# Maxima transposed in 64x64 tiles, self placement in two halves, cross scores in three units, on one Trainium2 core

## The chip, the cores and the metric

The kernel runs on one core of a Trainium2 chip. The metric is the device time of one execution, in microseconds. Three runs of the kernel before gave 484.20, 483.22 and 483.26 us, with a median of 483.26. In the profile, PE is TensorE (PEld its weight loads), DVE is VectorE, ACT is ScalarE, POOL is GpSimd and SP is SyncE; a q behind a name is that engine's sequencer, which also issues DMAs.

## What is computed

The reference is two transformer layers over x, of shape 4x512x128. Layer 0 is causal self attention with normalised q and k, cross attention to a context of 154 rows (16 heads of 8 features each), and a gated mixture of 8 experts. Layer 1 is causal linear attention, a second cross attention with 8 heads of 128 features, and a feed-forward block of 384 hidden features.

```python
def _L0_attn_ref(x, W_qkv, q_scale, k_scale, W_out):
    qkv = jnp.einsum('bsd,de->bse', x, W_qkv)
    q, k, v = jnp.split(qkv, 3, axis=-1)
    q = _layernorm(q, q_scale)
    k = _layernorm(k, k_scale)
    ...
    scores = jnp.einsum('bshd,bthd->bhst', q / jnp.sqrt(Hd).astype(q.dtype), k)
    scores = jnp.where(future[None, None, :, :], jnp.finfo(scores.dtype).min, scores)
    attn = jax.nn.softmax(scores, axis=-1)
...
x = _layernorm(x + _L0_attn_ref(...), axis=-1)
x = _layernorm(x + _L0_xattn_ref(x, ctx_1024, ctx_1024, ...), axis=-1)
x = _layernorm(x + _L0_ffn_ref(...), axis=-1)
x = _layernorm(x + _L1_attn_ref(...), axis=-1)
x = _layernorm(x + _L1_xattn_ref(x, ctx_1024, ...), axis=-1)
x = _layernorm(x + _L1_ffn_ref(...), axis=-1)
```

## The kernel before

Work is cut into steps such as (b, "S", a, g, u): batch b, self (a = 0) or cross (a = 1) attention, group g of four heads, unit u. One program-wide list of steps is written out by hand: `MERGE` is a string of letters, each of which takes the next step of one stream (s scores, t transposed scores, p products, r preparation of a batch, l placement, u setup, and so on), and `BANK_OF` gives each step its PSUM bank or its pair of banks. Every engine walks this list and does its own part of each step, in that order. Semaphores count how often a bank was filled and drained. So a table decides what each engine has queued behind what.

Attention of layer 0 runs in turns, one for each (b, a, g), in the order `TURNS`. In a turn TensorE makes the scores S in units, and VectorE reduces each unit to its negated row maxima. The maxima are cut into three bf16 parts in `mparts`; the step mT transposes these on TensorE, ScalarE copies the result to `mrows`, and SyncE places it by one DMA into the rows `MAX_ROWS` of Q6. Then TensorE makes the transposed scores ST, from which the placed rows have already taken the maxima, ScalarE takes exponentials into EX, PV multiplies them with the values, and cT transposes the products back for the division. Cross scores of a turn are eight pieces of 128 query rows by 154 context rows, two pieces to a unit, so four units; self scores are five units. Both use TensorE in tiles of 64x64.

Q and k enter as bf16 triples (a value, its rest and the rest of that) so that bf16 products are exact enough. After the step qkT, ScalarE and VectorE make the three parts of 128x512. A placing step then copies parts by DMA into every eighth partition of the operands Q6 and K6: twelve DMAs of 128 KB to a batch, six for q and six for k (`shares`, `placement`, `place_self`). At batch 0 SyncE issues six and ScalarE the other six (`place_first`), and the first scores wait for all twelve.

The head of the program loads x, the weights and the context (SyncE's list `early`, 15 loads, then the expert biases), computes qkv of batch 0, and makes setup transposes (wT) and products (wM) of weights. The first of these, wT 0 to 3, transpose the context of a batch. `keep_busy` puts a few products without use in front of the first x0T and the first qkv.

## Time and profile before

| | before |
|---|---|
| median of three runs | 483.26 us |
| the profiled execution's own time | 484.66 us |
| its span, first to last instruction | 482.9 us |
| granted TensorE clock, mean over the span | 0.975 |
| TensorE busy | 449.9 us (93%) |
| VectorE busy | 381.7 us (79%) |
| ScalarE busy | 346.9 us (72%) |
| GpSimd busy | 187.2 us (39%) |
| instructions | 14117 |

The profile is of one execution. A busy time is the sum over an engine's instructions; on TensorE these overlap and their ends are modelled, so a full TensorE isn't one at its peak. A stretch table gives each engine's busy time and number of instructions in a window, with the granted clock as a share of full speed, the share of time that the DMA engines are busy, and GB/s. In a timeline a row is start, duration, engine, line, operation, output and input, count, and in brackets the idle time before it with what ended it. A row of several instructions lasts from the first start to the last end.

### The profile page before, as it was taken

The page shows a single profiled execution, that of the slowest core. Times are in us where ns is not written, and L with a number is a line of the kernel's source. Part 1 is how long each engine was busy: PE and PEld are TensorE (multiplying, and loading weights), DVE is VectorE, ACT ScalarE, POOL GpSimd, SP SyncE. Part 2 cuts the span into 40 slices and gives each one's busy share as a digit, 9 for nine tenths or more (in the row PEclk, how much of TensorE's full clock was granted, in tenths as well). Part 3 has the DMA queues.
Part 4 walks back from the last instruction along what each step waited for, and adds up shares of the span by engine and source line. Part 5 has one row for each costly group of instructions (what it writes and reads, how often), then busy time and mean ns, then how long its engine had stood idle before and what let it go on. Part 6 is the DMA issues. An engine that isn't in the chain of part 4 may idle for free.

```text
span 482.9 us, 14117 instructions
## 1 busy us (share of the span) xinstructions
PE 449.9 (93%) x5296; PEld 303.5 (63%) x5296; DVE 381.7 (79%) x1083; ACT 346.9 (72%) x879; POOL 187.2 (39%) x356
## 2 busy tenths in 40 slices
PE   5767889998999999999999999999999999999995
PEld 4534446654555546656778555668774765896984
DVE  2469897898899999898698988867879687764566
ACT  1635676976868878888667788996867878869642
POOL 7284000680202364434142252335334538644532
PEclk8677999999999999999999999999999999999999
DMA  7481210034200201131100000030000000000001
GB/s 230 99 209 32 76 46 5 24 89 105 60 13 14 68 2 39 39 92 34 37 4 13 13 3 4 3 76 19 3 13 14 1 1 2 1 1 1 2 12 33
DMA packets 27191, 18.50 MB, mean 38 GB/s; under 512 B 8217, under 2 KB 26773, under 8 KB 26997
## 3 DMA queue, kind: packets, MB, share of 16 engines
q1 hardware_dynamic: 23413, 15.44, 12.1%
q10 hardware_dynamic: 3712, 2.17, 1.9%
q8 instruction: 43, 0.70, 0.6%
q14 instruction: 23, 0.19, 0.1%
HBM read 5.58 MB, written 1.05 MB: 14 GB/s over the span
## 4 chain that ended last, share of the span: by engine, by line
PE 46%; DVE 4%; ACT 2%; POOL 1%; issue 1%; POOLq 0%; DVEq 0%; ACTq 0%
PE psum L1070 6%; PE psum L1452 6%; PE psum L1429 5%; PE psum L1463 3%; PE psum L1365 3%; PE psum L1149 2%; PE psum L1474 2%; PE psum L1176 2%; PE psum L1219 2%; PE psum L1203 2%; PE psum L1454 1%; PE psum L1321 1%; PE psum L1326 1%; PE psum L1373 1%; PE psum L1207 1%
## 5 line engine op out<-in xcount | busy, mean ns | idle before, releaser
L1600 ACT ACTIVATE EX<-psum 128x1024 f32<-128x1024 f32 (+1 forms) x128 | 119.3, 975 | 7.2 <-PE psum L1131 4.2
L1873 DVE TENSOR_REDUCE mparts<-psum 128x2 f32<-128x768 f32 (+1 forms) x96 | 77.5, 862 | 3.4 <-PE psum L1131 3.0
L1868 DVE TENSOR_REDUCE mparts<-psum 128x4 f32<-128x616 f32 (+1 forms) x80 | 68.0, 877 | 4.8 <-PE psum L1149 3.6
L1028 POOL TENSOR_TENSOR GP<-REST,xrs 128x512 f32<-128x512 f32 (+1 forms) x48 | 34.6, 743 | 48.8 <-DVE xrs L2100 24.8
L1149 PE MATMUL psum<-K,Q 64*64 64x154 bf16 (+8 forms) x1024 | 48.1, 266 | 4.9 <-DVE mparts L1873 2.2
L1176 PE MATMUL psum<-Q,K 64*64 64x512 bf16 (+7 forms) x640 | 42.9, 313 | 3.4 <-DVE mparts L1873 1.5
L1689 ACT ACTIVATE REST<-psum,nxmax 128x154 f32<-128x154 f32 x96 | 36.2, 393 | 9.2 <-DVE nxmax L2090 8.2
L1149 PEld LDWEIGHTS psum<-K,Q 64*64 64x64 bf16 x1024 | 22.3, 106 | 28.0 <-issue 14.4
L1219 PE MATMUL psum<-EX,V 128*32 128x256 f32 (+3 forms) x512 | 37.8, 435 | 1.2 <-ACT EX L1600 1.2
L954 POOL TENSOR_SCALAR rstd_rest<-moments_rest 128x2 f32<-128x2 f32 x32 | 7.3, 228 | 73.2 <-DVE moments_rest L1908 72.8
L954 POOL TENSOR_SCALAR rstd_attn<-moments_attn 128x4 f32<-128x4 f32 x8 | 1.9, 238 | 82.1 <-DVE moments_attn L1908 82.1
L2090 DVE TENSOR_REDUCE nxmax<-psum 128x2 f32<-128x308 f32 x64 | 28.9, 470 | 4.6 <-PE psum L1429 4.1
L1429 PE MATMUL psum<-GP,xT 128*128 128x308 f32 x96 | 30.3, 431 | 0.1
L1176 PEld LDWEIGHTS psum<-Q,K 64*64 64x64 bf16 x640 | 15.4, 105 | 19.1 <-issue 5.6
L1219 PEld LDWEIGHTS psum<-EX,V 128*32 128x32 f32 x512 | 15.1, 109 | 18.8 <-issue 15.8
L1615 ACT COPY pvraw<-psum 128x512 f32<-128x512 f32 x16 | 9.4, 587 | 21.1 <-PE psum L1219 20.9
L1452 PE MATMUL psum<-VM,REST 128*128 128x128 f32 x192 | 23.8, 277 | 0.3 <-ACT EX L1600 0.2
L957 POOL TENSOR_TENSOR rstd_rest<-rstd_rest,power 128x2 f32<-128x2 f32 x32 | 22.9, 715 | 2.7
L1452 PEld LDWEIGHTS psum<-VM,REST 128*128 128x128 f32 x192 | 22.5, 192 | 1.1 <-issue 0.6
L1365 PE MATMUL psum<-ew,xT 128*128 128x512 f32 x48 | 22.7, 607 | 0.0
L1070 PE MATMUL psum<-ident,X 128*128 128x128 f32 x90 | 17.6, 294 | 5.1 <-DMA Y_rest<-in_ctx 3.7
L1070 PE MATMUL psum<-ident,pvraw 128*128 128x128 f32 x128 | 20.0, 279 | 1.4 <-ACT EX L1600 1.1
(344 smaller groups left out, 1151.3 us busy)
## 6 DMA issues: line engine op xcount, KB each, us to landing
Q<-xparts SPq DMA_DIRECT2D x24, 128.0 KB
Q<-parts SPq DMA_DIRECT2D x21, 128.0 KB
K<-parts SPq DMA_DIRECT2D x21, 128.0 KB
X<-in_x SPq DMA_DIRECT2D x4, 256.0 KB, 3.1
Q<-in_L_xattn_Wkv SPq DMA_DIRECT2D x1, 1024.0 KB, 7.2
K<-xkparts SPq DMA_DIRECT2D x24, 38.5 KB
out<-XB_rest SPq DMA_DIRECT2D x6, 128.0 KB, 1.8
Q<-in_L_xattn_Wq SPq DMA_DIRECT2D x1, 512.0 KB, 4.3
```

What stands on the lines that cost most here:

```text
L1028: last = nc.gpsimd.tensor_tensor(of.XP[:, at:at + 4 * n].rearrange("p (h c) -> p h c", h=4)[:, :, 0:c1 - c0], of.XE[:, :, c0:c1], of.xrs.r ...
L1070: last = nc.tensor.transpose(to[0:n, at:at + m], src, ident[0:m, 0:m])
L1149: last = mm(to[half, r, at:at + n], Q6[a][p, b % 2, 2 * g + jj, P * q + TILE * e:P * q + TILE * e + TILE], K6[a][p, b % 2, 2 * g + jj, 0:n ...
L1176: last = mm(to[half, r, at + q - P * k:at + S - P * k], K6[a][p, b % 2, 2 * g + jj, P * k + TILE * e:P * k + TILE * e + TILE], Q6[a][p, b ...
L1219: last = mm(to[32 * h:32 * h + 32, P * k:S], V[:, k, 4 * g + h, :], EX[:, ex_slot(b, a, g, u) + h % 2, at:at + n], start=k == PV_ORDER[0], ...
L1365: fills_(mm(fill(key), half_of(b, h).xT[2][:, P * i:P * i + P], ew[:, 4 * side:4 * side + 4, :].rearrange("p e d -> p (e d)")), key)
L1429: fills_(mm(fill(key)[:, 0:2 * C], half_of(b, h).xT[4][:, P * q:P * q + P], G[:, head:head + 2, :].rearrange("p h c -> p (h c)")), key)
L1452: mm(to, of.XPT[:, head, :], VM[:, head, :], start=head == 0, stop=False)
L1600: drains(nc.scalar.activation(dst, src, ACT.Exp), key)
L1689: last = nc.scalar.activation(of.XE[:, i, :], src[:, C * j:C * j + C], ACT.Exp, bias=of.nxmax[:, i:i + 1], accum_out=of.xsum[:, i:i + 1])
L1868: last = vec.tensor_reduce(nmax[:, :, :, q], src[:, :, 0:2 * n].rearrange("p r (j k) -> p r j k", j=2), AX.X, ALU.max, negate=True)
L1873: last = vec.tensor_reduce(nmax[:, :, jj, q], src[:, :, at:at + P * (q + 1)], AX.X, ALU.max, negate=True)
```

## The change

- The maxima of a turn are transposed by two 64x64 products with `ident2` (one for each half of the partitions), not by one transpose against a bf16 identity. `mrows` holds the two results at partitions 0 to 47 and 64 to 111, and two DMAs place them. The counts of `max_placed` double.
- Cross scores are cut into units of three, three and two pieces of 154 columns, and VectorE reduces a unit of cross scores by one instruction.
- The features of q and k are put in the order half, parity, feature, head, so that each half of the partitions holds the heads of two groups. A placement of a part becomes two DMAs of 64 partitions. At batch 0 the first halves go first (`first_placed`, six by SyncE and six by ScalarE), and the scores of groups 0 and 1 wait for these alone; SyncE issues the twelve second halves in the last placing step, and group 2 waits for them.
- Five of the 15 early loads and the two loads of the expert biases are issued in that last placing step, ahead of its second halves. The late loads of ScalarE are issued at batch 1's step qkT of q, not at its last qkv.
- The transposed gates `gT` and the biases `eb` have all 128 rows, with zeros below row 16, so the product of the gate biases runs over 128 rows.
- `cT` is cleared only in its last 32 columns, the bf16 identity goes, and one memset of `mparts` goes.
- `MERGE` and `BANK_OF` are new. The new order begins x0T, qkv 0 to 3, qkT 0 and 1 of batch 0, then wT 0; before, wT 0 stood ahead of qkv 0 and wT 1 to 5 ahead of qkT. Its moments of batch 1 stand behind the five units of the first scores; before, ahead of them.

```diff
-X_PIECES = [[(0, 0, q), (C, 1, q)] for q in range(NB)]
+X_COUNT = P * NB // C
+X_PIECES = [[(C * (i - first), i // NB, i % NB) for i in range(first, min(first + X_COUNT, 2 * NB))]
+            for first in range(0, 2 * NB, X_COUNT)]
...
 MERGE = (
-    "rurrrruuruuruwrrrllwllurrrrrusssssuvssssutrtstsrltstssspspttttlstprssplpsttssttstlup"
...
+    "rrrrrrrrrullwlluuwruuuursssrssrrrusussstrststtstvssrlptstusslptttpssrpssupttslttwslu"
...
+        def half_placement(b, w, s, part, y):
+
+            return (Q6, K6)[w][0][s:P:ROW_STEP, b % 2, NQ * y:NQ * y + NQ, :], parts[
+                TILE * y:TILE * y + TILE, w, part, :]
...
-        def placed_until(b):
-            return 16 * (2 * SLOTS * (b + 1) + max(0, b - 1))
+        def placed_until(b, a):
+            return 16 * (2 * SLOTS * (b + 1 if a else 2 * b + 1) + max(0, b - 1))
...
                 if b == 0 and y:
+
+                    if w:
+                        load_early(behind)
+                        sp.wait_ge(first_zeros_ready, 1)
+                        for m in range(2):
+                            sp.dma_start(eb[E * m:E * m + E, m, :], L0_ffn_expert_b
+                                         ).then_inc(eb_loaded, 16)
+                        for of in range(2):
+                            for s, part in (*shares(of, 0), *shares(of, 1)):
+                                sp.wait_ge(part_ready[0][part], 1 + of)
+                                sp.dma_start(*half_placement(0, of, s, part, 1)
+                                             ).then_inc(qk_placed, 16)
                     return
...
                     sp.wait_ge(part_ready[0][part], 2 * b + 1 + w)
-                    sp.dma_start(*placement(b, 0, w, s, part)).then_inc(qk_placed, 16)
+                    if b == 0:
+                        sp.dma_start(*half_placement(0, w, s, part, 0)
+                                     ).then_inc(first_placed, 16)
+                    else:
+                        for of in HALVES:
+                            sp.dma_start(*half_placement(b, w, s, part, of)
+                                         ).then_inc(qk_placed, 16)
...
                 if b or g:
-                    sp.wait_ge(max_placed[a], 16 * (NQ * b + g))
+                    sp.wait_ge(max_placed[a], 32 * (NQ * b + g))
                 drained(sp, (b, "mT", a, g))
-                sp.dma_start(Q6[a][MAX_ROWS, b % 2, 2 * g:2 * g + 2, :].rearrange(
-                    "p j t -> p (j t)"), mrows[:, parity(b, a, g), :]).then_inc(max_placed[a], 16)
+                to = Q6[a][MAX_ROWS, b % 2, 2 * g:2 * g + 2, :].rearrange(
+                    "p j (q h t) -> p (j q) h t", h=2, t=TILE)
+                for r in R:
+                    sp.dma_start(to[:, :, r, :], mrows[TILE * r:TILE * r + 48, parity(b, a, g), :]
+                                 ).then_inc(max_placed[a], 16)
...
-                if u == g == 0:
-                    pe.wait_ge(cross_placed if a else qk_placed, placed_until(b))
+                if a == b == u == g == 0:
+                    pe.wait_ge(first_placed, 16 * 2 * SLOTS)
+                elif u == 0 and g == (0 if a or b else 2):
+                    pe.wait_ge(cross_placed if a else qk_placed, placed_until(b, a))
...
-                fills_(nc.tensor.transpose(to[0:80, 0:64].bitcast(BF16),
-                                           high(mparts[:, parity(b, a, g), :]), identb[:, :]), key)
+                for r in R:
+                    p = slice(TILE * r, TILE * r + TILE)
+                    last = mm(to[TILE * r:TILE * r + 48, 0:TILE],
+                              high(mparts[p, parity(b, a, g), :]), ident2[p, :],
+                              start=True, stop=True)
+                fills_(last, key)
...
-                if len(pieces) == 2 and pieces[0][2] == pieces[1][2]:
+                if a:
+                    n, first = len(pieces), NB * pieces[0][1] + pieces[0][2]
+                    last = vec.tensor_reduce(
+                        three[:, :, 0, first:first + n],
+                        src[:, :, 0:n * C].rearrange("p r (m k) -> p r m k", m=n),
+                        AX.X, ALU.max, negate=True)
+                elif len(pieces) == 2 and pieces[0][2] == pieces[1][2]:
```

## Rows read from the trace of the kernel before

**Rows 1.** The page's first part: busy us, share of the span and instructions.

```profile
PE 449.9 (93%) x5296; PEld 303.5 (63%) x5296; DVE 381.7 (79%) x1083; ACT 346.9 (72%) x879; POOL 187.2 (39%) x356
```

**Rows 2.** The table of stretches: busy time and instructions, clock, DMA share, GB/s.

```profile
0.00:20.00 20.00, 12.96 (x44) 8.88 (x44) 6.38 (x30) 6.03 (x13) 12.01 (x28) 0.79 0.68 197
...
26.00:32.00 6.00, 4.33 (x16) 1.92 (x15) 2.38 (x16) 2.31 (x5) 5.77 (x5) 0.79 0.93 190
32.46:72.65 40.19, 31.24 (x603) 17.96 (x596) 37.93 (x64) 24.04 (x33) 9.44 (x16) 0.92 0.26 71
...
100.00:120.00 20.00, 17.54 (x327) 10.09 (x319) 17.44 (x35) 13.93 (x21) 7.19 (x10) 1.00 0.40 106
240.00:400.00 160.00, 158.57 (x1777) 107.19 (x1768) 131.81 (x418) 124.24 (x326) 59.92 (x130) 1.00 0.05 13
```

**Rows 3.** Timeline of the head, all engines and queues: start, us, what.

```profile
4.20 0.83 PE L1070 MATMUL psum<-ident,X 128*128 128x128 f32 x4
...
5.45 0.44 DVE L2126 COPY wqkv_p<-REST 128x128 f32<-128x128 f32 x1
...
8.75 0.18 PEld L1070 LDWEIGHTS psum<-ident,X 128*128 128x128 f32 x1 [3.96 <-DMA Y_rest<-in_ctx]
...
9.39 1.22 PE L1060 MATMUL psum<-ident 128*128 128x128 f32 x4
...
10.41 4.98 PE L1105 MATMUL psum<-wqkv_p,xT 128*128 128x384 f32 x8
...
18.21 0.66 SPq L831 DMA_DIRECT2D eb<-in_L_ffn_expert_b  x2
...
20.70 1.57 PEld L1070 LDWEIGHTS psum<-ident,qkn 128*128 128x128 f32 x8 [2.00 <-DVE qkn L1806]
...
24.74 0.58 ACT L1501 COPY xT<-psum 128x512 f32<-128x512 f32 x1
...
26.29 1.87 ACTq L1517 DMA_DIRECT2D K<-parts  x3
...
31.97 0.41 PE L1149 MATMUL psum<-K,Q 64*64 64x448 bf16 x4 [1.13 <-issue]
```

**Rows 4.** The same timeline, VectorE, ahead of the first maxima.

```profile
30.95 0.49 DVE L1786 BATCH_NORM_STATS2 qkstats<-qkn 128x6 f32<-128x128 f32 x2 [0.16 <-ACT qkn L1542]
31.47 0.64 DVE L1794 BATCH_NORM_AGGREGATE qkmoments<-qkstats 128x2 f32<-128x6 f32 x8
```

**Rows 5.** Groups of instructions by line and form: busy us, mean ns, idle before.

```profile
L1868 DVE TENSOR_REDUCE mparts<-psum 128x4 f32<-128x616 f32 x64 | 48.6, 792 | 3.8 <-PE psum L1149 3.6
L1873 DVE TENSOR_REDUCE mparts<-psum 128x2 f32<-128x1024 f32 x32 | 38.1, 1216 | 2.1 <-PE psum L1131 2.0
L1873 DVE TENSOR_REDUCE mparts<-psum 128x2 f32<-128x768 f32 x32 | 30.5, 952 | 1.3 <-PE psum L1131 1.1
...
L1228 PE MATMUL psum<-identb,mparts 128*80 128x128 bf16 x32 | 7.3, 227 | 1.8 <-DVE mparts L1883 1.8
```

**Rows 6.** Timeline around batch 1's placement: SyncE's queue, TensorE's scores.

```profile
56.87 0.78 SPq L806 DMA_DIRECT2D Q<-mrows  x1
58.84 0.40 PE L1176 MATMUL psum<-Q,K 64*64 64x512 bf16 x4
59.70 1.83 SPq L785 DMA_DIRECT2D K<-parts  x3
65.17 0.41 PE L1149 MATMUL psum<-K,Q 64*64 64x448 bf16 x4
```

**Rows 7.** Timeline of TensorE, two places behind 512-column products.

```profile
76.85 0.39 PE L1176 MATMUL psum<-Q,K 64*64 64x512 bf16 x4
77.06 0.22 PE L1131 MATMUL psum<-maskT,ident 64*64 64x128 bf16 x4
...
212.91 0.41 PE L1176 MATMUL psum<-Q,K 64*64 64x512 bf16 x4 [0.41 <-DVE mparts L1868]
213.25 0.77 PE L1070 MATMUL psum<-ident,GP 128*128 128x128 f32 x5
```

129 lines of the change are left out of this document (69 added, 60 removed).

## The prediction

> **What bounds the kernel now.** I read the page's busy shares first: TensorE is busy for 93% of the span and VectorE for 79% [rows 1]. A share over the whole span says little, so the second view is the table of stretches [rows 2]. It shows three stages. In the first 20 us TensorE works 12.96 us, at a mean granted clock of 0.79, and nothing else is full either; up to the first scores this is a chain of loads, normalisation and placement. From about 32 to 73 us VectorE is busy for 37.93 of 40.19 us (94%) while TensorE has 9 us to spare: the stage is bound by the maxima on VectorE. Later TensorE is full, for 158.57 of 160 us from 240 to 400: there only less TensorE work, or a later idle gap that closes, can shorten anything. One stretch inside that stage is looser, 100 to 120 us, with 17.54 busy. So there are about 2.5 us to win there, and most of the rest to be won lies before 80 us.
>
> The third view is the timeline of the head [rows 3], with the queues that issue DMAs. TensorE reaches the transposes of the context right after the first x0 transpose and waits 3.96 us for their load; only then come the four qkv products (start 10.41), although their weights were ready at 5.45 + 0.44 = 5.89. The normalised q and k are transposed at 20.70, the last of the twelve placing DMAs is issued at 26.29 + 1.87 = 28.16, and the first scores begin at 31.97, 3.8 us after that. From 26 to 32 us the DMA engines are 93% busy [rows 2]: the first scores wait for twelve DMAs of 128 KB in a backlog, not only for their latency.
>
> **The change, part by part.** The sum is made against the profiled execution, 484.66 us (span 482.90 and 1.76 around it). The median of the three runs is 483.26, so I take the differences from the one and put them on the other.
>
> *Order at the head.* The new order has x0 transpose, four qkv, qkT of q and of k, and only then the first context transpose. The qkv products can start when their weights are there (5.89) and the keep-busy products are done. Four of these instructions lie between 9.39 and 10.41 now, and in the new order they follow the x0 transpose, which ends at 4.20 + 0.83 = 5.03; with 1.2 us for them I take 6.3. That is 10.41 - 6.3 = 4.1 us earlier, and the chain behind it (copies, moments, root, normalisation, transposes, parts) moves as it is. SyncE must have its loads issued by then. It ends them at 18.21 + 0.66 = 18.9 now; five loads and the two of the expert biases, about 3 us of issuing, move behind the placement, so it is free near 15.9, ahead even of the transposes of q, which come at 20.70 - 4.1 = 16.6.
>
> *First placement in halves.* Twelve DMAs still have to be issued before the first scores, each of 64 KB. ScalarE has one more copy in front of its six (0.3 us), so the last is issued at 28.16 - 4.1 + 0.3 = 24.4. Half the bytes (0.79 MB for 1.57) leave no backlog. A row for the latency alone: a 12 KB placement of maxima issued until 57.65 is used at 58.84, 1.2 us later [rows 6]; with that and 3.8 as the ends, the scores could start between 25.6 and 28.2. But ScalarE has five copies for transposes to make after its DMAs (two of 512 columns at 0.58 us, three of 154, which I take at half that: 2.0 us), and a qkv product of batch 1 stands in front of the first scores and needs one of them. I take 26.8, a gain of 31.97 - 26.8 = 5.2 us at this point.
>
> *What the head no longer hides.* In the kernel before, VectorE takes the moments of batch 1 while the placement lands: four pairs of 0.49 and 0.64, 2.6 us, ending just before the first maxima [rows 4]. In the new order these stand behind all five units of the first scores. They become part of the VectorE-bound stage, so 2.6 of the 5.2 us come back at once.
>
> *Every self placement as two DMAs.* One issue takes 1.83/3 = 0.61 us [rows 6], and nothing in these rows makes it shorter for half the partitions; I take 0.6 as it is (0.3 if it went by bytes). Batches 1 to 3 issue 24 in place of 12, 7.3 us more of SyncE's queue each. For batches 2 and 3 the placement stands several turns ahead of its use. For batch 1 it doesn't. Now the last K part is issued at 61.53 and the scores of batch 1 begin at 65.17 [rows 6]: 3.6 us of slack, of which landing takes 1.2 to 2. Twelve issues for K last 7.3 us where six last 3.7, and the two DMAs for the maxima ahead of them take 0.8 more. So the slack turns into a wait of 7.3 - 3.7 + 0.8 + 1.2 to 2.0 - 3.6 = 2.0 to 2.8 us. The new order has a table conversion (about 0.8 us of VectorE) before these scores, which covers part: I take 1.8, with 0 and 3 as the ends. VectorE, which has nothing queued before those scores, waits with TensorE. Together the head gives -5.2 + 2.6 + 1.8 = -0.8 us.
>
> The Trainium skill (DMA: Bandwidth & Descriptors, Rules for kernel authors) speaks against this edit: of two transfers to disjoint partition halves it says not to bother, because they share the same engines and serialise. The change doesn't count on their running side by side at the first placement, since the second halves are issued later; for the placements of batches 1 to 3 the rule leaves only the cost, which is how they are priced above.
>
> *Maxima.* One transpose of 128x80 (227 ns [rows 5]) becomes two products of 64x64. A 64-column product is the smallest in the scores, and two tiles can overlap: I take no change, between -1 and +1 us over 32 turns. The copy on ScalarE reads 64 columns in place of 128. The second placing DMA puts 0.78 us [rows 6] between a turn's maxima and its transposed scores, 32 x 0.78 = 25.0 us if all of it showed. TensorE is in order, so scores queued behind a waiting transposed unit wait too, and VectorE behind them. Now the transposed scores come 1.97 us after the issue [rows 6], with as few as 4 steps of TensorE between; in the new table there are at least 7 in the first nine turns (5 in the very first). That is more than 0.78 us of work in most, so I take nothing, and keep 6 us as the bad end (eight turns fully open).
>
> *Tiles of TensorE.* Four 512-column products in 64x64 tiles take 0.21 us until the next work in the same tiles (76.85 to 77.06) and 0.34 until the next 128x128 work (212.91 to 213.25) [rows 7]: a change of tile shape costs about 0.13 us. Transposing the maxima in the tiles of the scores, and widening the gate bias product from 16 rows to 128, should save such changes, but counted over the new order they go from 306 to 314, because the steps are interleaved more finely. 8 x 0.13 = +1.0 us. The Trainium skill has the same rule (TensorEngine Tiling (Array Packing), Key Properties: changing the mode drains the engine); by itself it would make one expect a gain here, which the count takes away.
>
> *Cross scores in three units.* VectorE's reductions cost 1216, 952 and 792 ns for 1024, 768 and 616 elements [rows 5], so 1.04 ns an element and 0.15 us fixed. A cross turn now costs 4 x 0.792 = 3.17; with two of 924 elements (1.11) and one of 616 it is 3.02. Over 16 turns -2.4 us of VectorE, and 16 handovers less. These turns lie where TensorE is full, so I take half, -1.2 (0 to -2.4).
>
> *Where the new order puts TensorE's work.* Before the third maxima of batch 1 the new order has done xk, three qkv products of batch 2 and two transposed units that the old one does later, some 3 us, in a stage with TensorE idle. The gap that they can close is the 2.46 us of 100 to 120; I take half, -1.2 (0 to -2.5).
>
> The other edits (smaller memsets, no bf16 identity, late loads issued from another step, full-height gate transposes) cost POOL or ScalarE under 1 us where both have idle time; without that cover, up to 1 us.
>
> Sum: -0.8 + 0 + 1.0 - 1.2 - 1.2 = -2.2 us. 484.66 becomes 482.5, and on the median 483.26 - 2.2 = **481.1 us**.
>
> **Rivals.** *All of it carries.* The batch 1 scores don't wait (0 for 1.8), both tile and order terms are at their good ends: -5.2 + 2.6 - 2.4 - 2.5, and 0 for tiles, = -7.5, 475.8 us. For it: the first stage is a pure chain. Against it: TensorE is full later on.
> *The gain is turned into waits.* The head is won, but VectorE's 94% and the placement of batch 1 take it all, and the later terms come to nothing: -5.2 + 2.6 + 2.6 = 0, 483.3 us.
> *SyncE's queue becomes the bound.* A placing step now holds the queue for 6 x 0.61 = 3.7 us where it held it for 1.8, and the maxima of a turn that come behind it wait, then take two issues. It decides once the wait (up to 1.8 + 0.78 us) is longer than the work between a turn's maxima and its transposed scores. There are twelve such steps from batch 1 on; if four catch a turn fully (10.3 us) against a sum of -2.2 with half of it covered by other work, the result is 483.3 - 2.2 + 5.2 = 486.3 us. For it: SyncE's rows show the maxima already issued between placements; against it: turns of 10 us or more after 100 us. The skill's rule on halves, named above, points to this one.
> That the edits don't do what they say I leave out: the counts of the waits follow from the code.
>
> **How the numbers follow.** Forecast (478.5 to 482.3) 0.42; all carries (475 to 478.5) 0.17; waits (within 0.2%, 482.3 to 484.2, about what a measurement can tell from no change) 0.18; SyncE's queue or a worse order (over 484.2) 0.23. Faster 0.59, same 0.18, slower 0.23. The range is 475.5 to 486.0: some 3 in 100 lie below, 12 in 100 above.
>
> **What would show it.** Right: qkv near 6.3 us, first scores near 26.8, first maxima transposed 5 us earlier than now but the second only 2 to 3 us earlier; a wait of 1 to 3 us ahead of batch 1's scores, while SyncE issues K parts; cross reductions near 1.11 us; TensorE as full as now after 120 us. Wrong: first scores after 28 us; TensorE idle before transposed scores with the maxima's DMA as releaser; more than 3 us of TensorE idle between 120 and 400 us, or clearly less TensorE busy time than 449.9 us.

## The result, and the profile after

The kernel before took 483.73 us (median of four runs, 483.22 to 484.20) and the changed kernel 496.62 us (four runs, 493.92 to 497.64): a ratio of 1.026, interval 1.021 to 1.030. The change costs 12.9 us where 2.2 us of gain were forecast, and the result lies far outside the range. The profiled execution took 497.64 us, span 495.9, mean granted clock 0.963. (Of the runs further down, one execution of e8 lies outside everything else, at 1059.33 us with a full granted clock, and nothing on record explains it; e8's median of 481.38 counts it, that of its four others is 481.26.)

First the page: busy times, and the granted clock in 40 slices of 12.4 us.

```profile
## 1 busy us (share of the span) xinstructions
PE 454.0 (92%) x5328; PEld 303.7 (61%) x5328; DVE 382.3 (77%) x1066; ACT 345.9 (70%) x879; POOL 187.5 (38%) x356
...
PEclk9596989998989999999999999999999999999999
```

TensorE's busy time grew by 4.1 us against [rows 1], part of it at a lower clock, and VectorE's by 0.6. The span grew by 13.0 us. So most of the loss is waiting. The table of stretches shows where; its first row is the kernel before, the others the changed one:

```profile
60.00:80.00 20.00, 17.60 (x348) 10.26 (x341) 18.24 (x34) 14.06 (x21) 0.00 (x0) 1.00 0.13 33
...
60.00:80.00 20.00, 14.54 (x245) 7.50 (x249) 13.16 (x25) 10.74 (x16) 0.00 (x0) 0.91 0.10 30
...
120.00:140.00 20.00, 15.81 (x298) 8.85 (x298) 16.57 (x34) 11.40 (x19) 3.81 (x8) 1.00 0.24 75
...
240.00:400.00 160.00, 157.79 (x1876) 106.70 (x1873) 127.88 (x373) 122.61 (x312) 57.32 (x121) 1.00 0.07 18
```

From 240 to 400 us TensorE is nearly as full as before (157.79 us busy for 158.57 [rows 2]). From 60 to 80 us both engines are loose: 14.54 us of TensorE and 13.16 of VectorE in 20, for 17.60 and 18.24 before. The stage bound by VectorE has become one in which VectorE waits:

```profile
DVE mparts L1873 <- PE psum L1131: 3.0, 8, 0.6
DVE mparts L1868 <- PE psum L1149: 3.6, 8, 0.9
...
DVE mparts L1921 <- PE psum L1160: 18.4, 15, 7.3
DVE mparts L1910 <- PE psum L1180: 5.9, 8, 1.7
```

That is the waits view, two rows of the kernel before and two of the changed one: total, number of waits, longest. In the changed kernel most reductions of self scores (L1921) waited 18.4 us for TensorE in 15 waits. The longest, 7.3 us, is the head, before the first scores; the other 14 are 11.1 us, for 3.0 us before (L1873). Those of cross scores waited 5.9 us (L1910) for 3.6 (L1868). I also followed one marker through all kernels: when ScalarE copies the transposed maxima of a turn. Each number below is its start in a kernel minus its start in the kernel before, in us, one column per turn shown (each from that kernel's timeline).

```text
turn                    1     2     3     4     5     6     8     9    11    16    24    32
changed kernel       -6.3  -5.0  -2.0  -0.3   3.1   6.6   4.0   7.4   9.5  10.2  14.4  13.0
e11 (no halves)      -6.1  -4.8  -2.1  -0.4  -0.8   4.1   1.5   3.3   5.4   4.8   9.0   7.6
e13 (gaps filled)    -6.4  -5.4  -3.7  -0.4   3.0   6.5   3.9   5.8   9.4  10.1  14.3  12.8
e9  (late loads)     -0.4   2.8   4.7   4.7   4.7   4.6   4.6   6.3   6.3   6.3   6.3   6.3
e15 (small edits)    -0.5   2.5   5.1   5.1   5.1   5.0   5.0   5.0   6.0   6.0   6.0   5.9
e5  (+ halves)       -1.1   1.8   3.9   3.9   8.3   8.3   8.3   8.5  15.3  15.3  15.3  15.2
e6  (+ three units)   0.1   2.7   5.1   5.1   5.1   5.1   5.1   5.2   5.3   5.7   7.5  10.6
e7  (+ two products) -0.9   3.0   4.3   4.2   4.7   5.1   5.3   6.6   7.9   8.1   9.2  10.7
e8  (head alone)     -2.6  -2.3  -2.3  -2.3  -2.3  -2.3  -2.3  -2.3  -2.5  -2.5  -2.4  -2.5
e17 (old, then new)  -4.2  -4.1  -4.2  -4.2  -4.2  -4.2  -4.2  -2.8  -0.6  -1.7   2.6   1.5
e18 (new, then old)  -5.7  -4.4  -2.5   0.9   1.4   4.9   2.3   7.8   7.7   7.7   7.7   7.7
```

The changed kernel is 6.3 us ahead at the first turn. At the ninth it is 7.4 behind and at the eleventh 9.5. The head paid, and the ten turns behind the first lost 16 us. The first eight turns hold self scores alone: the first cross unit is reduced at 114.96 us, behind the eighth turn. So what is lost up to there (10.3 us in the changed kernel, 7.6 in e11) can't come from the three cross units. The timeline of the head (start, duration, row, idle time before):

```profile
5.94 2.85 PE L1134 MATMUL psum<-wqkv_p,xT 128*128 128x384 f32 x8
...
14.12 1.97 PE L1099 MATMUL psum<-ident,qkn 128*128 128x128 f32 x8 [5.33 <-DVE qkn L1848]
...
19.77 1.85 ACTq L1557 DMA_DIRECT2D K<-parts  x3
...
25.59 0.60 PE L1180 MATMUL psum<-K,Q 64*64 64x448 bf16 x4 [0.23 <-issue]
```

The qkv products start at 5.94 us, where 10.41 stood in [rows 3], and the first scores at 25.59, where 31.97 stood. TensorE had stood idle for only 0.23 us ahead of them: they came behind a qkv product of batch 1, and no longer behind a wait for the placement. Next, the place that the forecast had named, ahead of batch 1's scores:

```profile
56.58 9.10 SPq L819 DMA_DIRECT2D K<-parts  x12
...
67.18 0.64 PE L1180 MATMUL psum<-K,Q 64*64 64x448 bf16 x4 [2.37 <-DMA K<-parts]
...
67.93 3.55 DVE L1921 TENSOR_REDUCE mparts<-psum 128x2 f32<-128x1024 f32 x4 [2.98 <-PE psum L1160]
```

SyncE needs 9.10 us for twelve half K parts, 0.76 each on average; I had taken 0.61 from [rows 6]. Undisturbed, six halves take 3.78 us in this same kernel (at 114.63 us), 0.63 each, so some 1.5 us of the 9.10 is hold-up in between, whose cause no run shows. The last is issued at 65.68 and used 1.5 us later. TensorE waits 2.37 us and VectorE 2.98. For the two DMAs that place the maxima, TensorE's transposed scores waited only 0.6 us in the whole program.

### The profile page after: what moved, and what is told of

Its sections match the earlier page's. It is cut to its first block, busy times and chain, and to the rows that moved or that the text cites. A ratio compares the mean times of both kernels' runs of the same rounds, so it can differ in the third digit from the quotient of the medians.

```text
span 495.9 us, 14247 instructions
## 1 busy us (share of the span) xinstructions
PE 454.0 (92%) x5328; PEld 303.7 (61%) x5328; DVE 382.3 (77%) x1066; ACT 345.9 (70%) x879; POOL 187.5 (38%) x356
## 4 chain that ended last, share of the span: by engine, by line
PE 41%; DVE 6%; ACT 3%; POOL 2%; issue 2%; POOLq 0%; DVEq 0%; ACTq 0%
PE psum L1099 6%; PE psum L1487 5%; PE psum L1464 5%; PE psum L1498 3%; PE psum L1400 3%; PE psum L1207 2%; PE psum L1250 2%; PE psum L1509 2%; PE psum L1180 2%; PE psum L1234 2%; PE psum L1489 1%; PE psum L1356 1%; PE psum L1238 1%; PE psum L1282 1%; DVE mparts L1910 1%
## 5 line engine op out<-in xcount | busy, mean ns | idle before, releaser
L1642 ACT ACTIVATE EX<-psum 128x1024 f32<-128x1024 f32 (+1 forms) x128 | 121.0, 981 | 17.7 <-PE psum L1160 12.0
L1921 DVE TENSOR_REDUCE mparts<-psum 128x2 f32<-128x768 f32 (+1 forms) x96 | 78.2, 861 | 18.7 <-PE psum L1160 18.4
L1910 DVE TENSOR_REDUCE mparts<-psum 128x6 f32<-128x924 f32 (+1 forms) x48 | 47.2, 1003 | 6.1 <-PE psum L1180 5.9
L1207 PE MATMUL psum<-Q,K 64*64 64x512 bf16 (+7 forms) x640 | 44.6, 321 | 7.8 <-DVE mparts L1921 3.0
L1057 POOL TENSOR_TENSOR GP<-REST,xrs 128x512 f32<-128x512 f32 (+1 forms) x48 | 33.3, 715 | 40.6 <-DVE xrs L2148 26.9
L1731 ACT ACTIVATE REST<-psum,nxmax 128x154 f32<-128x154 f32 x96 | 36.6, 407 | 11.1 <-DVE nxmax L2138 10.7
L1250 PE MATMUL psum<-EX,V 128*32 128x256 f32 (+3 forms) x512 | 38.9, 444 | 0.2
L1160 PE MATMUL psum<-maskS,ident 64*64 64x128 bf16 (+2 forms) x320 | 22.0, 239 | 0.0
L1731 ACT ACTIVATION_READ_ACCUMULATOR REST<-psum,nxmax 128x1 f32 x96 | 21.3, 222 | 0.0
```

The source lines that it names most:

```text
L1057: last = nc.gpsimd.tensor_tensor(of.XP[:, at:at + 4 * n].rearrange("p (h c) -> p h c", h=4)[:, :, 0:c1 - c0], of.XE[:, :, c0:c1], of.xrs.r ...
L1207: last = mm(to[half, r, at + q - P * k:at + S - P * k], K6[a][p, b % 2, 2 * g + jj, P * k + TILE * e:P * k + TILE * e + TILE], Q6[a][p, b ...
L1250: last = mm(to[32 * h:32 * h + 32, P * k:S], V[:, k, 4 * g + h, :], EX[:, ex_slot(b, a, g, u) + h % 2, at:at + n], start=k == PV_ORDER[0], ...
L1642: drains(nc.scalar.activation(dst, src, ACT.Exp), key)
L1731: last = nc.scalar.activation(of.XE[:, i, :], src[:, C * j:C * j + C], ACT.Exp, bias=of.nxmax[:, i:i + 1], accum_out=of.xsum[:, i:i + 1])
L1910: last = vec.tensor_reduce(three[:, :, 0, first:first + n], src[:, :, 0:n * C].rearrange("p r (m k) -> p r m k", m=n), AX.X, ALU.max, nega ...
```

## Experiments

All of these compute everything the reference asks for. The kernel before ran beside each group of runs, with medians of 484.13 to 484.86 us. Below, "+8.7" means the median of a run minus that of the kernel before in the same group. The intervals of the ratios are 0.2 to 0.5% to either side (0.7% for e13), so a difference under 1.5 us between two kernels, and one under 3 us where e13 or e14 is one of them, is not told apart.

**1. Code or order?** The order table and the code were exchanged, and two parts were taken out of the changed kernel.

```diff
 # e1_old_order: changed code, table of before
-    "rrrrrruuuurr..."
+    "rurrrruuruur..."   # fourth cross units struck
 # e2_new_order: code of before, new table, a fourth cross unit put behind each third
 # e3_full_place: changed kernel, whole placing DMAs, scores wait for all twelve
-                        for of in HALVES:
-                            sp.dma_start(*half_placement(b, w, s, part, of)
+                    sp.dma_start(*self_placement(b, w, s, part)).then_inc(qk_placed, 16)
 # e4_one_mT: changed kernel, the maxima as before
-                for r in R:
-                    sp.dma_start(to[:, :, r, :], mrows[TILE * r:TILE * r + 48, parity(b, a, g), :]
+                sp.dma_start(Q6[a][MAX_ROWS, b % 2, 2 * g:2 * g + 2, :].rearrange(
```

> The changed kernel with the step order and the banks of the kernel before (the fourth cross unit of each turn struck out of them). If the new tables are the cause, 480 to 487 us, since the rest of the change stays. If the doubled DMAs are (placements of batches 1 to 3 and of the maxima), it stays at 490 to 500: the rows of the kernel before show only 3.6 us between batch 1's last K part and its scores in this order, and six more issues take 3.7.

> The kernel before with the new step order (a fourth cross unit put behind each third). If the new tables are the cause, 493 to 500 us with the old DMAs. If the doubled DMAs are, 478 to 485: the head comes about 6 us earlier for the scores less what the backlog of full placements takes (1 to 2 us), and no wait of 2.4 us stands ahead of batch 1's scores.

> The changed kernel with each part of self q and k placed by one DMA of 128 partitions, as before, and all scores of batch 0 waiting for all twelve. If the doubled placements are the cause, the 2.4 us wait and the 3 us of VectorE idle time ahead of batch 1's scores go, TensorE's clock stays up from 60 to 80 us, and the time falls to 484 to 489. If the tables are, it falls by at most 3 us, to 492 to 497, and the first scores come 1 to 2 us later than 25.6.

> The changed kernel with the maxima transposed by one 128x80 transpose and placed by one DMA, as before. If the second DMA's 0.8 us a turn is what is paid, 6 to 12 us come back (484 to 490). If it is hidden, as the prediction had it, within 2 us of the changed kernel (494 to 498).

Measured: e1 510.38 us (+26.2, ratio 1.055, 1.052 to 1.058), e2 528.17 (+44.0), e3 492.86 (+8.7, ratio 1.019, 1.015 to 1.022), e4 496.52 (+12.3, ratio 1.025, 1.022 to 1.028). The second product and the second DMA of the maxima cost nothing on the new order. In e3 and e4 the second value of each expectation came: halves aren't the whole cause, and the maxima's second DMA is hidden. Halves cost 3.8 to 4.2 us there: with whole DMAs the wait of 2.37 us is gone, and by the marker e3 stands at 0.0 at the fifth turn, where the changed kernel is at 3.1. In e1 and e2 both values of the expectations were missed by 10 us and more: neither table suits the other's code, so an exchange says little of the order's own worth. In e2 the bank pairs of the fourth units were my choice, and TensorE waited 15.6 us for banks that VectorE held, so I draw nothing more from it.

In the first group the prediction's third rival turned up, but in e1: TensorE's waits for the maxima's DMA.

```profile
PE psum L1207 <- DMA Q<-mrows: 8.7, 7, 6.2
```

**2. One part at a time on the old order.** The changed code, the table of before, and one large part each. e15 has none of them and is the base of the other three.

```diff
 # all four: table of before, four cross units (but e6), one product and DMA for maxima (but e7),
 # whole placing DMAs (but e5)
-X_COUNT = P * NB // C
...
+X_PIECES = [[(0, 0, q), (C, 1, q)] for q in range(NB)]
```

> The changed code on the step order and banks of the kernel before, with four cross units and one transposed product for the maxima: of the large parts only the placement in halves is left (beside the small edits: smaller memsets, a gate bias product over 128 rows, five loads and the expert biases issued later). My theory: the halves cost queue time of SyncE, as full placement won 3.8 us on the new order. On the old order the last K part of batch 1 has 3.6 us of slack of which landing takes at least 1.2, and twelve issues for K take 3.7 us more than six, so a wait of 2 to 3 us ahead of the first scores of batch 1; the first scores of all gain 2 to 3 us from half the bytes. I expect 483.7 + 1 = 484.7 us (483 to 488). Rival: the small edits or the halves themselves hold the rest of the loss (9 us); then it is above 490.

> The changed code on the order and banks of the kernel before, with the fourth cross unit left out of the order, full placement and one transposed product for the maxima: only the three cross units are left (beside the small edits). The same order with halves and two products gave 510.4 us, 26.6 more than the kernel before. My theory: an order written for four units doesn't fit three. A unit of two banks now holds three pieces and its bank pair is drained later, the turn's last unit is missing where the order had a product to cover it, and TensorE waits for banks and maxima; the three units are then worth most of the 26.6 us: I expect 500 us (495 to 510). Rival: three units are what the prediction made of them, a small gain, and the 26.6 us come from halves and the second product on an order without room for them: then it is 483.7 - 1.2 = 482.5 us (481 to 486) and the run with two products, or that with halves, shows the loss.

> The changed code on the order and banks of the kernel before, with four cross units and full placement: only the two products and two placing DMAs for the maxima are left (beside the small edits). The second DMA holds the queue 0.78 us more for each of 32 turns. In the old order there are as few as 4 steps of TensorE between a turn's maxima and its transposed scores, and at least 7 in the new one. My theory: a part of it shows where the order is short: I expect 483.7 + 4 = 487.7 us (484 to 495). Rival: it is hidden as on the new order, where one product in place of two changed nothing: 483.7 within 1 us.

> The changed code on the order and banks of the kernel before with none of its large parts: whole placing DMAs, one transposed product and one DMA for the maxima, four cross units. Left are the small edits: late loads behind ScalarE's part of q of batch 1 (5.6 us alone), five loads and the expert biases behind the first placement, gate bias product and its operands over 128 partitions, memsets. My theory: the late loads carry nearly all: 484.1 + 5.6 = 489.8 us (489 to 491). Then, on the old order, halves cost 499.1 - 489.8 = 9.3 us, three units 4.3 and the maxima's two products 4.4. Rival: the other small edits cost too, up to 494, and the large parts (except halves) nothing.

Measured: e15 490.24 (+5.4), e5 499.07 (+14.9), e6 494.11 (+10.0), e7 494.22 (+10.1). So on the old order the small edits cost 5.4 us, halves 9.5 more, three units 4.6 and the two products 4.7 (these cross two groups of runs). The expectations for e5 to e7, written before e15, had put the small edits at nothing: e5 came out 14 us above its value, e7 at the top of its range, and e6 just below the range of its theory (495 to 510). The four together make 24.2 us of the 26.2 that e1 cost, which has them all. The turns in the table above show where each loses. Halves lose at the fifth turn (batch 1's placement) and, 7 us, at the eleventh (batch 2's). The timeline of e5 there:

```profile
126.92 3.77 SPq L818 DMA_DIRECT2D K<-parts  x6
127.68 0.26 ACT L1645 COPY mrows<-psum 48x128 bf16<-48x128 bf16 x1
130.74 2.70 SPq L840 DMA_DIRECT2D Q<-mrows  x2
132.71 0.64 PE L1205 MATMUL psum<-Q,K 64*64 64x512 bf16 x4 [5.13 <-DMA Q<-mrows]
```

The maxima were ready at 127.94, their DMA was queued behind six K issues until 130.74, and the transposed scores used it at 132.71, after TensorE had stood still for 5.13 us. Of these, 2.80 are the queue's. That is the mechanism of the third rival, fully open. In the changed kernel the new order keeps these apart, and TensorE's waits on that DMA are 0.6 us in all.

Three units lose slowly over the cross turns, from 5.2 at the ninth turn to 10.6 at the last. The reduction itself is what I had worked out. The view of line 1910 in the changed kernel gives shortest, median and longest in ns:

```profile
L1910 DVE TENSOR_REDUCE mparts<-psum x48: 783/1110/1121, 115.0 to 376.5; 128x6 f32<-128x924 f32 x32, 128x4 f32<-128x616 f32 x16
```

In e6 this order only had its fourth units struck, its banks were not chosen anew for three. So the 4.6 us are the cost of three units on a table made for four; what three units cost as such no run shows.

**3. The small edits.** The turns of e5, e6 and e7 all lost 5 us from the first to the third, so one of the small edits was suspect: the six late loads that ScalarE issues.

```diff
 # e9_before_late: kernel before, with the edit of the change
-                if b == 1 and n == NB - 1:
-                    load(late)
...
+                if b == 1 and w == 0:
+                    load(late)
 # e10_after_late, e11_after_late_full: changed kernel (e11 with whole placing DMAs)
             def exponentials(b, a, g, u):
+                if a == b == g == u == 0:
+                    load(late)
```

> The kernel before with one edit of the change alone: the six late loads that ScalarE issues (30.45 to 33.5 us, in a wait) are issued behind ScalarE's part of q of batch 1, as in the change, which is at about 46 us, between exponentials. In the changed kernel the six issues last 45.80 to 48.98 and the exponentials, which TensorE's products wait for, stop for 2.59 us. All three runs with one part of the change on the old order lost 5 us from the second to the third turn, 44.7 to 49 us. My theory (a queue held in a critical place, which the prediction had costed at under 1 us): 483.9 + 4.5 = 488.4 us (487 to 489.5), with the loss in place by the fourth turn and constant after it. Rival: the 5 us of those runs come from their other parts and the loads are hidden: 483.9 to 484.9.

> The changed kernel with the six late loads issued before ScalarE's first exponential, where it waits 3.79 us (34.14 to 37.93 us), in place of 45.80 to 48.98. My theory: the exponentials of the second turn come up to 2.6 us earlier and with them the turns behind; between the third and the sixth turn the changed kernel lost 10 us against before, and about 3 of these come back: 496.6 - 3 = 493.5 us (492 to 495). Rival: the stage is bound by its order and the placement, not by ScalarE, and it stays within 1 us of 496.6.

> As the run before this one, and with whole placing DMAs of 128 partitions for self attention (which alone gave 492.9 us). My theory: the two losses are of different places (ScalarE at 46 us, SyncE and the DMAs at 56 to 68 us) and add: 492.9 - 3 = 490 us (488.5 to 491.5), which leaves 6 us for the order. Rival: both edits open the same wait, of the scores of batch 1, and together give no more than the better: 492.5.

Measured: e9 489.78 (+5.6, ratio 1.011, 1.008 to 1.014), e10 495.71 (+11.5), e11 492.48 (+8.3). The one moved line costs 5.6 us in the kernel before, as much as all small edits together (e15). Its timeline:

```profile
44.84 0.34 ACTq L1520 DMA_DIRECT2D gw<-in_L_ffn_gate_w  x1
...
47.78 0.84 ACTq L1520 DMA_DIRECT2D REST<-in_L_ffn_w_down  x1
48.66 1.02 ACT L1600 ACTIVATE EX<-psum 128x1024 f32<-128x1024 f32 x1 [3.14 <-issue]
...
49.74 0.64 PE L1149 MATMUL psum<-K,Q 64*64 64x448 bf16 x4 [2.65 <-ACT EX L1600]
```

ScalarE issues six DMAs in a row and makes no exponential meanwhile. A bank that an exponential should free stays full, TensorE waits 2.65 us for it, and VectorE 1.43 us behind it. In the changed kernel the same issues stand at 45.80 to 48.98, with a gap in the exponentials as well:

```profile
45.80 0.34 ACTq L1560 DMA_DIRECT2D gw<-in_L_ffn_gate_w  x1
...
49.08 1.94 ACT L1642 ACTIVATE EX<-psum 128x1024 f32<-128x1024 f32 x2 [2.59 <-PE psum L1160]
```

Yet there they cost 0.9 to 1.4 us by the medians (e10), which these runs hardly tell from nothing, and 0.4 once halves are out (e11 against e3): my expectation of 3 us fell, its rival held. I read this as a stage that already waits for something else; e11 against e10, with the loads moved in both, puts halves at 3.2 us.

**4. TensorE's clock.** In the changed kernel TensorE stood still for 2.53 us up to 37.18, and its granted clock was 0.50 (the level of 1.2 GHz) from 36.2 to 46.5 us: it fell during the standstill. TensorE stood still again for 2.37 us up to 67.18, and the clock was low from 67.0 to 70.4. (These ends are worked out from stretches of 2 us; the expectations have them up to 1.4 us later.) e13 and e14 put products without use into these gaps, e16 into the gap of the head-only kernel (part 5).

```diff
 # e13_fill, and e14_full_fill on e11
+                if a == b == g == u == 0:
+                    drained(pe, (1, "qkv", 1))
+                    keep_busy(bank((1, "qkv", 1)), 12)
...
+                if b == 1 and a == u == g == 0:
+                    drained(pe, (0, "ST", 0, 2, 3))
+                    keep_busy(bank((0, "ST", 0, 2, 3)), 12)
 # e16_head_fill, on e12
+                if a == b == g == 0 and u == 3:
+                    drained(pe, (1, "x0T", 0))
+                    keep_busy(bank((1, "x0T", 0)), 13)
```

> The changed kernel with twelve products without use (128x128 fp32, some 0.17 us each at full clock, 2.0 us together) in each of the two places where TensorE stands still for over 2 us: before the first transposed scores (34.66 to 37.18 us) and before the first scores of batch 1 (64.81 to 67.18). They write banks that nobody reads then. My theory: the half clock follows these gaps; with them filled, the 11 us at half clock from 36.9 and the 5 us from 67 go, TensorE's 8 us of work there take half the time, VectorE's waits of 2.98 us and 1.4 to 1.9 us shrink, and the kernel gains 3 to 5 us: 496.6 - 4 = 492.6 us (491 to 494.5). Rival: the order bounds the stage, the clock goes along without effect: within 1 us of 496.6, even if the granted clock rises.

> The changed kernel with whole placing DMAs and the late loads in a wait (492.5 us), and the same two groups of twelve products. There the wait ahead of the scores of batch 1 is gone, so the second group has no gap and costs up to 2 us of TensorE, while the first acts as in the run before. My theory (clock): 492.5 - 4 + 1 = 489.5 us (488 to 491.5). Rival (order): 492.5 to 494.

> The kernel before with the new head order and the late loads on SyncE (481.0 us), and thirteen products without use in the one gap of over 2 us that it has, before the fourth unit of the first scores (28.48 to 31.15 us). Now the clock is at half from 32.7 to 38.7 us, but VectorE is busy for 19.7 of the 20 us from 28 to 48. My theory: the half clock goes away and nothing is gained, as VectorE bounds the stage: 481.0 (480.3 to 481.6). Rival: the slow stretch costs here too: 479.5 or less.

Measured: e13 496.69 (+11.8), e14 495.35 (+10.5), e16 481.67 (-3.2). The stretch from 38 to 47 us, first in the changed kernel and then in e13, and under them e13 from 62 to 64:

```profile
38.00:47.00 9.00, 8.19 (x112) 4.30 (x108) 6.34 (x13) 5.72 (x7) 5.26 (x7) 0.53 0.03 4
```

```profile
38.00:47.00 9.00, 6.79 (x134) 3.23 (x124) 7.37 (x15) 5.46 (x8) 5.16 (x7) 1.00 0.11 17
...
62.00:64.00 2.00, 2.00 (x19) 1.67 (x19) 0.96 (x4) 1.50 (x2) 0.00 (x0) 0.50 0.33 110
```

The granted clock in the first stretch rose from 0.53 to 1.00, and TensorE did more instructions in less busy time. At the third turn e13 is 1.7 us ahead of the changed kernel (-3.7 and -2.0), but at the fourth and fifth it is where that one is (-0.4 and -0.3, 3.0 and 3.1). So the low clock of that stretch costs nothing that reaches the fourth turn. The test of the second stretch is not clean: a low stretch from 60.1 to 67.0 us took the place of the one from 67, and the products without use took 4.06 us (from 64.59) for a gap of 2.37. In e14, where the second gap doesn't exist, the kernel came out some 2 us above e11 and above both values of its expectation, which is within the noise of the two. Over all runs the clock as the main cause falls: e14 has no low stretch from 36 to 47 us and is no faster than e11. What the later low stretches cost (111.4 to 114.8 and 142.1 to 145.5) wasn't tried.

**5. The head alone.**

```diff
 # e8_head_only, on the kernel before
-    "rurrrruuruuruwrrrllwllurrrrr..."
+    "rrrrrruuuurrrllwllwruuurrrrr..."
...
+                    if w:
+                        load_early(behind)
 # e12_head_late_sp: also
-                    load(late)
...
+                        for dst, src in late:
+                            sp.dma_start(dst, src).then_inc(late_loaded, 16)
```

> The kernel before with the order of its first steps alone changed: x0 transpose, four qkv, moments, then the context transposes, qkT of q and k, the placement as before with whole 128 KB DMAs, and the five late loads and expert biases issued after that. From batch 1 on everything is as before; the moments of batch 1 stay ahead of the first scores. The changed kernel got its qkv at 5.94 us in place of 10.41 and its first scores at 25.6 in place of 31.97. My theory: the head's chain carries: qkv near 6, first scores near 28 (a backlog of whole DMAs stays), first maxima transposed 3 to 4 us earlier, and as the stage up to 73 us is bound by VectorE without a gap and the later stages by TensorE, most of that reaches the end: I expect 483.7 - 3 = 480.7 us (479.5 to 482.5). Rival: the earlier start is lost again in the stages behind it, as in the changed kernel, where 17 us were lost from the first maxima to the turn at 138 us: then it is 483.7 or above.

> The kernel before with the new order of its first steps (481.4 us alone) and the six late loads issued by SyncE behind the expert biases, at 24.4 to 28 us, where its queue is free until 37 us, in place of ScalarE at 28.37 to 32.98. There a copy on ScalarE comes 33.02 behind a wait on issues and TensorE waits 0.85 us for it, while VectorE's maxima bound the stage. My theory: ScalarE's copies come up to 2 us earlier, but the stage is bound by VectorE, so 0 to 1 us: 481.0 (480 to 481.6). Rival: the loads now share the DMA engines with the placement that the first scores wait for (they are busy for 93% there in the kernel before), and it is 482 us or more.

Measured: e8 481.38 (-2.8, ratio 0.994, 0.992 to 0.997), e12 481.03 (-3.1, ratio 0.995, 0.993 to 0.997). Both beat the kernel before and the changed one; between the two no difference can be told. The timeline of e8:

```profile
6.07 3.47 PE L1110 MATMUL psum<-wqkv_p,xT 128*128 128x384 f32 x8
...
23.15 5.17 PE L1110 MATMUL psum<-wqkv_p,xT 128*128 128x384 f32 x8 [4.12 <-ACT xT L1506]
...
28.69 0.41 PE L1154 MATMUL psum<-K,Q 64*64 64x448 bf16 x4
```

First scores come at 28.69 for 31.97, and the turns stay 2.3 to 2.6 us ahead to the last. What is won in the head reaches the end, within the noise one for one, if the order behind it is left as it is. The whole DMAs are not why this is 28.69 and not 25.59: in e3, which has them too, the first scores begin at 26.49, after an idle time of 1.50 us. In e8 they stand behind the qkv products of batch 1, for which TensorE waited 4.12 us on a copy by ScalarE.

**6. Which half of the new order?** Both orders have done nearly the same steps at the eighth turn's maxima, so they can be joined there.

```diff
 # e17_old_then_new: order of e8 up to (1, "mT", 0, 3), then the new one (three cross units)
 # e18_new_then_old: new order up to there, then that of before (four cross units)
 # both: changed code, whole placing DMAs, one product and DMA for the maxima
# late loads: in e17 at their old place, in e18 before the first exponential
```

> Changed code with whole placing DMAs, one transposed product and one DMA for the maxima and the late loads at their old place. Its order is that of the kernel before (with the new first steps) up to the maxima of the eighth turn, and from there the new order with its three cross units. Theory (the loss lies mainly behind the eighth turn): the eighth maxima come 2.4 us earlier than before, and the rest loses 6 us as it does in the changed kernel with whole placement (1.5 us late at the eighth turn, 7.6 at the last): 484.2 - 2.4 + 6.1 = 487.9 us (486.5 to 489.5). Rival (the loss lies in the first eight turns, and what follows only carries it): 484.2 - 2.4 - 1.2 for three units = 480.6 us (480 to 482).

> The same code with four cross units and the late loads before the first exponential. Its order is the new one up to the maxima of the eighth turn and that of the kernel before from there. Theory: the eighth maxima are 1.5 us late, and nothing is lost behind it: 485.7 us (484.5 to 487). Rival (the loss is in the first eight turns): 490 to 492, as the changed kernel with whole placement, 492.5.

Measured: e17 488.21 (+4.0, ratio 1.009, 1.007 to 1.010), e18 491.37 (+7.1, ratio 1.015, 1.012 to 1.018). In e17 the theory's value came (487.9, the loss behind the eighth turn), in e18 the rival's (490 to 492, the loss in front of it), so neither story was right alone: each half costs. Up to the eighth turn e17 is 4.2 us ahead. Against e8, the new order with three units from there on costs 6.8 us by the medians; by its own marker e17 loses 5.7 behind the eighth turn, in a profiled run that was the fastest of its five. The new first part, which has the new head in it, ends up 7.1 us behind. Together that is more than the 8.3 us that both halves cost in one kernel (e11): e18 loses 5.5 us between the eighth and the ninth turn, e11 1.8. So some 4 us of e18 belong to the seam.

What happens in the first part can be read in e11's timeline, from the fifth turn's maxima on (between the fifth and the sixth turn e11 loses 4.9 us by the marker):

```profile
72.94 0.41 PE L1166 MATMUL psum<-K,Q 64*64 64x448 bf16 x4 [0.45 <-ACT EX L1626]
...
73.44 2.40 DVE L1905 TENSOR_REDUCE mparts<-psum 128x2 f32<-128x1024 f32 x2 [1.70 <-PE psum L1148]
...
75.53 3.21 PE L1236 MATMUL psum<-EX,V 128*32 128x512 f32 x32
...
78.67 0.36 PE L1166 MATMUL psum<-K,Q 64*64 64x320 bf16 x6
...
79.19 2.48 DVE L1905 TENSOR_REDUCE mparts<-psum 128x2 f32<-128x768 f32 x4 [2.87 <-PE psum L1148]
```

VectorE has nothing to reduce for 1.70 us: the first scores of the turn stand behind transposed scores and then wait 0.45 us for a bank that an exponential still holds. TensorE then has two units of scores for it (2.40 us of work), and behind them a products step of 3.21 us. VectorE waits 2.87 us more for the third unit. Part of this is the clock: it was 0.50 in e11 from 73.9 to 77.3 us, and 1.00 in the kernel before. The same turn in the timeline of the kernel before:

```profile
73.64 0.41 PE L1149 MATMUL psum<-K,Q 64*64 64x448 bf16 x4
...
74.13 2.36 DVE L1873 TENSOR_REDUCE mparts<-psum 128x2 f32<-128x1024 f32 x2 [0.44 <-PE psum L1131]
74.26 2.36 PE L1219 MATMUL psum<-EX,V 128*32 128x512 f32 x32
...
77.07 1.29 DVE L1873 TENSOR_REDUCE mparts<-psum 128x2 f32<-128x768 f32 x2 [0.58 <-PE psum L1131]
```

Its first scores come right behind the maxima's transpose, the products take 2.36 us at the full clock, and VectorE waits 0.44 and 0.58 us. From 65 to 106 us VectorE worked 35.85 of 41 us before, and 31.91 in e11. I read this as the cost of the order's banks and of long steps between a turn's units, with up to 0.85 us (3.21 - 2.36) of the clock in it; no run changed this one place by itself, so it is read from the trace, not shown.

## Why the prediction was wrong, and where it was right

*Head order and first placement* (a gain of 5.2 us at the first scores, taken back in part by 2.6 us of moments). Right, and even low: 6.4 us were won there, 6.3 at the first maxima. By e3 (first scores at 26.49) some 5.5 of the 6.4 are the order, for which I had 4.1, and 0.9 the half placement, for which 1.1 was left. Two errors inside met, which is luck: q's transposes came at 14.12 (16.6 forecast), so all parts were issued by 21.6 and not 24.4, but the first scores were then held by TensorE's own steps and not by the landing. Where the moments were to take back 2.6 us at once, 1.3 of the lead had gone at the second turn and 4.3 at the third, with the late loads in between. That a gain there can reach the end is shown by e8.

*Halves* (1.8 us, between 0 and 3, ahead of batch 1). Right place and mechanism, wrong size: 3.8 to 4.2 us. The term was mis-sized twice. The twelve issues took 9.10 us where I had 7.3. And I let the table conversion cover part of the wait, but VectorE still waited 2.98 us. The Trainium skill's advice (DMA: Bandwidth & Descriptors, Rules for kernel authors) not to split a transfer into partition halves agrees with the trace here: e3, with whole transfers, is faster by 3.8 us. The Trainium skill gives as its reason that both halves share the same DMA engines; what the trace shows as the cost is SyncE's time for twice as many issues.

*Two products and two DMAs for the maxima* (0). Right on the new order, by e4. On the old order, with as few as 4 steps between a turn's maxima and its transposed scores, the same edit costs 4.7 us. That the short distance is the reason is not shown: TensorE waited 2.8 us for this DMA in e7 and 2.0 in e15, 0.8 us of the 4.7.

*Three cross units* (-1.2). The duration was right (1110 ns measured, 1.11 us estimated), so by that sum 2.4 us of VectorE's work did go. The gain was not borne out: VectorE waited 5.9 us for these scores where it had waited 3.6, and the part of the new order with these units cost 6.8 us (e17). The units and their order weren't tried apart on a table made for both.

*Where the new order puts TensorE's work* (-1.2, between 0 and -2.5). This is the step that failed, and the largest. I asked only which gap of TensorE the moved work could close and gave the term no bad end. Instead of closing a gap the new order opened some: in the first eight turns, where VectorE had been the bound, e11 loses 7.6 us, and VectorE works 31.91 us from 65 to 106 us where it worked 35.85. Whole placing DMAs leave 8.3 to 8.7 us of loss (e11, e3), and neither the late loads nor the maxima account for it, nor the one low stretch of the clock that was filled. So, by elimination, it is the new order with its banks and cross units, in the first eight turns the steps and banks alone. (The moved moments of batch 1, 2.3 us of VectorE's work there, are in these 7.6 us.)

*Other edits* ("under 1 us where both have idle time"). Wrong where it stood: I named no cover for ScalarE at the new place. It is 5.6 us on the old order (e9) and 0.9 to 1.4 on the new one (e10).

*Tile switches* (+1.0). Not measured by itself.

*The rivals.* "The gain is turned into waits" had the mechanism and ended at 0, since it counted only one wait. "SyncE's queue becomes the bound" is real on the old order (5.13 us in one place) and absent from the changed kernel. Of the signs listed beforehand, the wait ahead of batch 1, the 1.11 us and the early qkv and first maxima came true; the second maxima came 5.0 us earlier and not 2 to 3. The one for "wrong" that came true is TensorE idle between 120 and 400 us: 4.19 us in the first 20 of these alone and 10.0 in all. As a sign it was badly set, since the kernel before already had 4.05 there.

Of the 12.9 us, halves are about 4 and the late loads about 1. The remaining 8 are what is left of a larger loss once the head's 6 us are taken off: e11 loses 7.6 us in the first eight turns, where no cross unit is involved, and 6.1 behind them. How the first divides between steps and banks, and the second between steps, banks and units, stays open.

## What to carry to other kernels

A gain at the head of a program reaches the end only if the stage behind it is not touched: e8 kept its 2.8 us, while the full change was 6.3 us ahead at its first turn and 9.5 behind at the eleventh. In a stage bound by one engine, cost a reordering by how long that engine's next input is delayed at each step, with the banks that it needs and who still holds them, not by the busy time that the edit saves. A run of DMA issues is work of the engine that issues it: before moving it, find a wait of that engine as long as the issues, as every later instruction of it, and a bank that it should free, stands behind them.

## What the runs showed of the hardware that I had not expected

A DMA of half the partitions costs as much of the queue as a whole one. Six halves (64 KB each) in the changed kernel, then six whole ones (128 KB) in e3:

```profile
114.63 3.78 SPq L819 DMA_DIRECT2D Q<-parts  x6
...
55.89 3.80 SPq L808 DMA_DIRECT2D K<-parts  x6
```

That is 0.63 us each in both. TensorE's granted clock fell to its lower level within standstills of 2.53 and 2.37 us, and after the first it stayed there for 10.3 us, although TensorE was busy for 8.19 of 9 us in it. Filling the gap took that stretch away, another one appeared from 60.1 us on, and the time didn't change. In e16, a full clock from 32 to 40 us where e12 had the low one from 32.6 to 39.4 gave nothing either (481.67 against 481.03); VectorE was busy for 19.16 of 20 us from 28 to 48 us in e16.
